# A two-layer attention kernel: a second tile for h1's copy and for h2, and every engine's order written out anew

## The reference

```python
# layer 0, per item
h  = rmsnorm(x) ;  h1 = x  + attention(h, h)            # "sa": 16 heads of 16, 256 keys
hn = rmsnorm(h1);  h2 = h1 + attention(hn, context)     # "ca": 77 keys
hn = rmsnorm(h2);  h3 = h2 + (silu(hn @ gate) * (hn @ up)) @ down     # inner width 1024
# layer 1, per item: norm_F = layernorm(h3), norm_X = layernorm(context)
a  = softmax(norm_F @ norm_X.T / 16) @ norm_X
c  = gelu(a @ fc1.T + fc1_b) @ fc2.T + fc2_b            # inner width 4
s  = attention of layernorm(c) with itself, one head
out = norm_F + gamma2 * (c + gamma1 * s)
```

## Time and profile before

| | us |
|---|---|
| median of 3 runs (lowest, highest) | 937.34 (936.94, 937.65) |
| span of the profiled execution | 938.1 |
| PE busy, weight loads busy | 869.7, 738.1 |
| DVE busy, ACT busy, POOL busy | 666.7, 546.2, 252.9 |
| mean granted TensorE clock | 0.984 |

### The profile page before, as it was taken

One profiled execution on the slowest core, in us unless ns is written; L12 is line 12 of the kernel. 1 busy time (PEld: TensorE's weight loads), 2 busy tenths in 40 slices (PEclk: granted clock), 3 DMA queues, 4 the chain that ended last, 5 costly groups with the idle time before them and its releaser, 6 DMA issues.

```text
span 938.1 us, 21220 instructions
## 1 busy us (share of the span) xinstructions
PE 869.7 (93%) x8114; PEld 738.1 (79%) x8114; DVE 666.7 (71%) x1445; ACT 546.2 (58%) x1098; POOL 252.9 (27%) x511
## 2 busy tenths in 40 slices
...
PEclk9899999999999999999999999999999999997999
...
GB/s 207 191 148 128 134 76 81 61 105 26 57 101 43 94 64 80 79 81 56 102 38 55 104 44 95 63 81 77 80 55 92 50 43 105 43 33 35 17 12 23
DMA packets 74660, 71.73 MB, mean 76 GB/s; under 512 B 17633, under 2 KB 67409, under 8 KB 74561
## 3 DMA queue, kind: packets, MB, share of 16 engines
...
...
## 4 chain that ended last, share of the span: by engine, by line
PE 74%; DVE 12%; ACT 6%; issue 3%; DMA 2%; SPq 1%; POOL 1%; ACTq 0%; DVEq 0%
PE mring L1527 21%; PE ring L1527 12%; PE down_ps L1667 9%; PE od L1634 9%; PE ring L1620 7%; PE ring L1600 6%; DVE mx_sa L1296 4%; PE ring L1535 2%; PE mring L1696 1%; PE mring L1769 1%; DVE late_a L1343 1%; ACT probs L1094 1%; PE ring L1607 1%; PE mring L1677 1%; DMA pk_sa<-qkT 1%
## 5 line engine op out<-in xcount | busy, mean ns | idle before, releaser
L1094 ACT ACTIVATE probs<-ring 128x1024 f32<-128x1024 f32 (+1 forms) x192 | 190.9, 1022 | 45.3 <-PE ring L1620 41.5
L849 POOL TENSOR_TENSOR hidT_lo<-late_a,hidT_hi 128x256 fp32r<-128x256 f32 x128 | 95.8, 750 | 316.9 <-ACT hidT_hi L1121 315.7
L1296 DVE TENSOR_REDUCE mx_sa<-ring 128x4 f32<-128x1024 f32 x128 | 153.4, 1215 | 11.4 <-PE ring L1600 11.3
L1301 DVE TENSOR_REDUCE mx_ca<-ring 128x4 f32<-128x308 f32 x128 | 55.1, 474 | 59.8 <-PE ring L1600 59.7
L1349 DVE SCALAR_TENSOR_TENSOR late_a<-late_a,mring 128x256 f32<-128x256 f32 x128 | 52.9, 413 | 49.1 <-ACT late_a L1111 48.7
L1667 PE MATMUL down_ps<-down_hi,hidT_hi 128*128 128x256 f32 x256 | 79.0, 309 | 0.0
L1111 ACT ACTIVATE late_a<-mring 128x256 f32<-128x256 f32 x128 | 48.4, 378 | 51.2 <-PE mring L1527 48.9
L1600 PE MATMUL ring<-pk_sa 63*128 63x256 f32 x512 | 62.8, 329 | 14.9 <-DVE mx_sa L1296 6.4
L1667 PE MATMUL down_ps<-down_lo,hidT_hi 128*128 128x256 f32 x256 | 71.3, 279 | 0.0
L1667 PE MATMUL down_ps<-down_hi,hidT_lo 128*128 128x256 f32 x256 | 71.3, 279 | 0.0
L1121 ACT ACTIVATE hidT_hi<-late_a 128x256 fp32r<-128x256 f32 x128 | 52.6, 413 | 27.0 <-DVE late_a L1351 19.9
...
## 6 DMA issues: line engine op xcount, KB each, us to landing
...
```

The lines of the kernel that those rows point to most:

```text
L849: nc.gpsimd.tensor_tensor(hidT[1][:, m % HID, :], hid[:, m % 2, :], hidT[0][:, m % HID, :].bitcast(F32), ALU.subtract).then_inc(S["hidlo"] ...
L1094: nc.scalar.activation(granule(g, tag)[0:rows_, i0:i0 + 2, :, :].rearrange("p i h t -> p h i t"), ring_tile(("E", tag, k))[0:rows_].rearra ...
L1296: nc.vector.tensor_reduce(mx[tag][:, :, :, k].rearrange("p q h -> p h q"), ps[:].rearrange("p h (q t) -> p h q t", t=T), AX_X, ALU.max).th ...
L1301: nc.vector.tensor_reduce(mx[tag][:, :, half, 2 * C * (k % 2) + k // 2:2 * C * (k % 2) + k // 2 + C + 1:C].rearrange("p q i -> p i q"), v, ...
```

## The change

- `h1_ca` gets a second tile (`h1_odd`), h2 a second one in `v_all`, which is free after the start. Even items use the first, odd items the second. The two waits above now look two items back.
- `ORDER` holds every (step, item) of every engine; `MOVED` and the sorting are gone. The steps are the same. Of TensorE's 1105, 784 have another place in the list, mostly by one to ten places.
- `MOVED_TILES` gives 62 `ring` and 91 `mring` fills the other PSUM tile.
- `IDLE` has 167 identity products, 100 of them ahead of items 0 to 2 (55 before) and 67 near the end (41 before).
- `w5_sb` shares the space of `lpT`.

Below, the lines of ORDER for DVE and TensorE around item 6 stand for the whole text; the start of ACT's and of DVE's list follow.

```diff
+ORDER["dve"]: S.sa.0@6 S.sa.1@6 o.ca.1@4 hv@0 wo.sa@5
+        oT.ca@4 S.sa.2@6 aT.ca@4 S.sa.3@6 ms.ca@5 wo.ca@4 s2@2 ms.mlp@4 xn.ca@5 xn.mlp@4 S.sa.4@6 T.mlp@4 S.sa.5@6 S.sa.6@6 u2@2 S.sa.7@6
+        maxsplit.sa@6 T.ca@5 gu.0@4 gu.1@4 ms.sa@7 lnstat.nx@4 qk.ca@5 dn@3 lnstat.nf@3 lncen.nf@3 gu.2@4 gu.3@4 S.ca.0@5 S.ca.1@5 sc@3 S.ca.2@5
...
+ORDER["pe"]: S.sa.0@6 S.sa.1@6 pv.ca.1@4 wo.sa@5 nXT@3 dnp.3@3 xT@2 S.sa.2@6 S.sa.3@6
+        dnp.4@3 dnp.5@3 dnp.6@3 wo.ca@4 s2@2 v.sa@6 mT2@2 S.sa.4@6 e2@2 dnp.7@3 T.mlp@4 u2@2 S.sa.5@6 S.sa.6@6 gu.0@4 S.sa.7@6 T.ca@5 gu.1@4 maxT.sa@6
+        qk.ca@5 gu.2@4 E.sa.0@6 E.sa.1@6 gu.3@4 E.sa.2@6 pv.sa.0@6 E.sa.3@6 E.sa.4@6 dnp.0@4 nFT@3 dnp.1@4 S.ca.0@5 S.ca.1@5 fT@2 sc@3 E.sa.5@6
...
+ORDER["act"], start: gT.0@0 norm.sa@0 ws.0@0 ws.1@0 T.sa@0 ws.2@0 norm.sa@1 ws.3@0 ws.4@0 ws.5@0 qk.sa@0
-    start before:    ws.0@0 gT.0@0 ws.1@0 ws.2@0 ws.3@0 norm.sa@0 ws.4@0 gk.0@0 gv.0@0 T.sa@0 ws.5@0 kt@0 gT.1@0 ws.6@0 qk.sa@0
+ORDER["dve"], start: gT.0@0 ms.sa@0 xn.sa@0 T.sa@0 ws.0@0 ws.1@0 ws.2@0 ws.3@0 ws.4@0 ws.5@0 qk.sa@0 S.sa.0@0
-    start before:    gT.0@0 ws.0@0 ws.1@0 km@0 ws.2@0 ws.3@0 ms.sa@0 ws.4@0 xn.sa@0 gk.0@0 T.sa@0 ws.5@0 gT.1@0 ws.6@0 qk.sa@0 kt@0 S.sa.0@0
...
+        h1_at = (h1_ca, sb("h1_odd", [P, QT, D]))
+        h2_at = (h2, v_all[:].rearrange("p q h e -> p (q h e)")[:, 0:QT * D].rearrange("p (q d) -> p q d", q=QT))
...
             def h1_for_ca(n):
                 act.wait_ge(S["sa", "res"].sem, S["sa", "res"].at(n, 1))
-                if not_first(n):
-                    act.wait_ge(S["ca", "res"].sem, S["ca", "res"].at(n - 1, 1))
+                if not_first(n, 2):
+                    act.wait_ge(S["ca", "res"].sem, S["ca", "res"].at(n - 2, 1))
...
-                nc.scalar.activation(h1_ca[:], h1[:], ACT.Copy).then_inc(S["h1"].sem, 1)
+                nc.scalar.activation(h1_at[n % 2][:], h1[:], ACT.Copy).then_inc(S["h1"].sem, 1)
...
-                src, dst = (x_res, h1) if tag == "sa" else (h1_ca, h2)
+                src, dst = (x_res, h1) if tag == "sa" else (h1_at[n % 2], h2_at[n % 2])
...
-                if tag == "ca" and not_first(n):
-                    dve.wait_ge(S["h3"].sem, S["h3"].at(n - 1, 1))
+                if tag == "ca" and n == 1:
+                    dve.wait_ge(s_vst, 16 * moves(len(GROUPS) - 1))
+                if tag == "ca" and not_first(n, 2):
+                    dve.wait_ge(S["h3"].sem, S["h3"].at(n - 2, 1))
```

More of the change, by code:

```diff
@@ L67 @@
[L67 to L70, removed]
+        gT.0@0 norm.sa@0 ws.0@0 ws.1@0 T.sa@0 ws.2@0 norm.sa@1 ws.3@0 ws.4@0 ws.5@0 qk.sa@0 ws.6@0 ws.7@0 gv.0@0 ws.8@0 ws.9@0 gk.0@0 v.sa@0 gT.1@0
@@ L79 @@
     "pe": """
[L80 to L83, removed]
@@ L309, in sequence, with step_of @@
[L309 to L326 removed]
+def step_of(word):
+    name, *args = word.split(".")
+    return (name, *(int(a) if a.isdigit() else a for a in args))
```

459 lines of the change are left out of this document (276 added, 183 removed), and 70 rows, old and new, of the table MOVED.

## The result

The changed kernel takes 929.08 us (median of 4 runs, 926.74 to 931.43), the kernel before 937.5 beside it: a ratio of 0.9907, interval 0.9884 to 0.993. It is faster, by 8.4 us. The forecast was 24 us, so the gain is a third of what was forecast. Two more measurements of the same kernel gave 928.23 and 927.28 us (ratios 0.9895 and 0.9897). Its 14 single times run from 922.5 to 935.9 us with a standard deviation of 3.9 us; the 68 of the kernel before run from 933.6 to 945.1 with 2.0. That wider spread turns out to be part of the story.

The account below looks back on a forecast made before the run. DVE's list was taken to bound the S stretch (S.sa.0 to maxT.sa done), some 40% of each item, PE the rest. Middle -16, start -5, end -3 give -24: 914.1 us span, 913.3 us time; forecast 906 to 922, 8-in-10 range 900 to 936.

Parts of the forecast that it names:

- The start, -5: Up to S.sa.0 of item 2: earlier norm.sa, ms.sa and xn, later gk, gv and fold; -5 us, ends -12 and +3.
- The whole shift and the identity products keep the clock: Best case for the start: qk.sa's full shift of at most 5.7 us counts and the clock holds; -12 us.
- The middle, -16: S stretches (S.sa.0 to maxT.sa done), items 2 to 15: three quarters of -21.5 us of DVE work and waits; ends -25, 0.
- DVE's list sets the S stretch: From S.sa.0 to maxT.sa done, some 40% of each item, DVE's work is the bound: busy 18.39 of 19.95 us.
- -12.0 us for dn and gu.0: DVE work leaving the S stretches: dn -6.8, gu.0 -8.3, less what enters; free in the other stretch.
- -9.5 us for the covered rstd waits: xn.ca and ms.ca between ms.mlp and xn.mlp cover two thirds of DVE's 1.02 us idle per item, 14 items.
- this is not a third gain: ACT running norm.ca ahead of norm.mlp, with mT2 and v.sa behind it, falls in the same S stretches; no extra gain.
- Its signs: If right: S stretches 18.0 to 18.9 us, DVE over 90% busy or PE without waits; wrong if 19.5 or more.
- Partly given back: Rival, 0.20: PE becomes the bound as its covers shrink; 8 to 12 us lost over 14 items, time 922 to 935.
- mT2 to e2: In that rival: PE work between these two kernel steps shrinks from 2.2 to 0.3 to 0.7 us; about 0.9 needed.
- Slower through mring: Rival, 0.10: 78 more consecutive fills on one PSUM tile wait for readers; 952 us at 0.5 us each.
- The end, -3: From wo.ca to T.mlp of items 14 and 15: more cover, 2 us wait and perhaps 2 us cold clock; ends -8, +1.

Follow-up runs that it names:

- after_b: The changed kernel unaltered, measured a third time: 927.28 us, ratio 0.9897.
- idle_both: Changed kernel with the 19 identity products of item 1 put back and those at the end as before (41, not 67): 926.75 us, ratio 0.9878.
- idle_item1: Changed kernel with the 19 identity products that the kernel before had in item 1 put back: 925.01 us, ratio 0.9835.
- half_before: Kernel before with the sa maxima taken over half of the keys, so DVE has less to do: 932.31 us.
- dn_late: Kernel before plus second tiles; in items 5 to 13 dn goes behind u2 on DVE, dnp.0 to just before dnp.1 on TensorE: 944.24 us, 1.0062.
- dve_part: Kernel before, second tiles; items 5 to 13: dn, dnp.0 and gu.0 later, h1, norm.ca, ms.ca and xn.ca earlier: 962.58 us.
- h1_early: Kernel before, second tiles; items 4 to 13: h1, norm.ca ahead of norm.mlp on ACT, ms.ca, xn.ca earlier on DVE: 940.44 us, 1.0021.
- cover1: Kernel before, second tiles; items 5 to 13: dn and dnp.0 later, dnp.7 moved between S.sa.4 and v.sa on TensorE: 942.43 us.
- after_again: The changed kernel unaltered, measured a second time: 928.23 us, ratio 0.9895.
- after: The changed kernel itself, first measurement and profile: 929.08 us, ratio 0.9907 to the kernel before.
- tail_idle: Changed kernel with the identity products at the end as in the kernel before (41, not 67): 925.66 us.
- half_after: Changed kernel with the sa maxima taken over half of the keys, so DVE has less to do: 917.95 us.
- idle_item1_b: Second measurement of the changed kernel with the 19 identity products of item 1 put back: 923.19 us.
- old_head: Old order and identity products up to S.sa.0 of item 2, the changed kernel's order, tiles and products from there on: 927.86 us.

## Why the prediction was wrong, point by point

- **The sum.** In the first profile the parts are +4.3, -7.1 and -5.7 us for -5, -16 and -3: the start and the middle each miss by some 9. The forecast took the clock of the kernel before as given outside the start and the end ("the granted clock is at full speed in nearly all slices"). It was not given: the missing products cost 5 to 8 us in item 1, and the low clock at 755 some 3 us in the first profile (item 14 takes 54.9 us, 52.0 in after_b). idle_both's parts are -2.8, -13.5 and -7.6, together -23.9 for -24. That agreement is luck. It is the fastest of six executions of a kernel with other products, set against a usual one of before; no part agrees by itself, and the middle's reason is wrong. At equal clock the changed kernel is 12 to 13 us faster, not 24 (below).
- **The clock and the times.** Changed kernel 922.5 us at a mean clock of 0.988, 928.5 at 0.979 and 935.9 at 0.970; before, 937.5 at 0.985, 938.8 at 0.978 and 945.1 at 0.968. A straight line through all executions gives 7.4 us for 0.01 of clock in the changed kernel (14 executions) and 4.4 before (64 of known clock). At 0.984 the lines give 925.3 and 937.4, at 0.988 922.4 and 935.7. That the fuller TensorE makes the low clock dearer fits this; it was not tested.
- **The start, -5: the step that failed.** "The whole shift and the identity products keep the clock" was counted as a chance of more gain. The new list has none of the 19 products of item 1, and the prediction only added up the totals, 100 for 55. It priced the products by the time that they take (0.24 us each) and put what they protect at nothing. It measured +2.0 to +5.7 us for -5 (113.3, 115.6 and 117.0 for 111.3), and -2.6 to -3.0 with the 19 products. The shift itself was right: S.sa.0 of 0 at 26.2 for 30.96. The Trainium skill (GPSIMD Engine Reference, section Key points) says that GpSimd shares its SBUF interfaces with VectorE. By that rule `fold` would take time back in item 1, 2 us by the prediction. It does not: the one operation of DVE beside it with two SBUF inputs, aT's low part (L1360), took 0.70 us for 0.69 before (0.78 in idle_item1), and sa_wo's split, now away from `fold`, 0.68 for 1.09.
- **The middle, -16: the mechanism was wrong.** It measured -7.1, -8.6 and -11.0 us in the changed kernel, -13.5 in idle_both. The step that failed is "DVE's list sets the S stretch", from 18.39 us busy in 19.95. DVE waited in between for what TensorE did in its own order, and 4.2 us of DVE work less shortened a stretch by 0.3 (half_before). -12.0 us for dn and gu.0: dn is worth 0 (dn_late), gu.0 was not parted from its tile (dve_part). -9.5 us for the covered rstd waits: DVE's idle time before xn.mlp did fall, from 10.6 us in 14 stretches to 3.3, as forecast, but such waits give 0.2 us a stretch (h1_early), some 3 us in 14. As far as the gain is explained, it comes from places in TensorE's list, of v.sa above all (cover1), and of v.sa and mT2 the prediction had said that "this is not a third gain".
- **Its signs did not part the theories.** DVE busy for over 90% of the S stretches, the wait before xn.mlp gone, ACT's wait for the residual sum down by over half (56.9 to 22.5 us), the weight-load share at 82%, S.sa.0 of 0 at 26.2, the clock at 1.00 from wo.ca of 14 on: all came true, and they hold as well if TensorE's order sets the stretch. The S stretches themselves, 19.1 us, fell between its two signs (up to 18.9, or 19.5 and more). Of the signs against it one came true, the longer start, though not "for `fold` and the later splits".
- **Partly given back.** This rival held in part. The other stretches of items 3 to 14 did not grow while the transfers were in time (some 379.6 us in idle_both for 380.1) and grew by 1.6 us in after_b. Excess rose ahead of S.ca.0 (0.6 us before, 2.7 in idle_both, 4.5 in after_again, in 12 items), ahead of qk.ca (0.2 to 2.1, from T.ca, a cover that the prediction had named) and, inside the S stretches, ahead of wo.ca (0.3 to 3.5). Two other named covers, nFT to sc and mT2 to e2, were not it. S.ca.0 of 11 in after_b and in idle_both:

```profile
648.46 0.52 PEld L1633 LDWEIGHTS ring<-kpk_ca,qpk_ca 63*128 63x128 f32 x8 [1.60 <-DMA qpk_ca<-qkT]
```

```profile
641.86 0.52 PEld L1635 LDWEIGHTS ring<-kpk_ca,qpk_ca 63*128 63x128 f32 x8 [0.41 <-issue]
```

The third packing transfer of ca of 11 lands 4.6 us after its issue in after_b and 2.7 in idle_both, and in the changed order it has no cover left. This is no chance of one execution: it takes 4.5 to 4.6 us in all five profiles of the changed order without the products in item 1 (after, after_again, after_b, tail_idle, half_after) and 2.7 in the other four that have the changed middle (idle_both, idle_item1, idle_item1_b, old_head). In the five, a 16 KB packet of the instruction queue (q8) takes 0.9 us on the DMA engines between issue and landing; in the four it is over before the issue. No experiment moved that packet alone.
- **Slower through mring.** It did not happen; 78 more pairs of fills on one tile cost nothing that shows in TensorE's waits. dve_part shows that the mechanism is real: 1.5 us a pair once the reader is late.
- **The end, -3.** Right in kind, mis-sized: -5.7 to -8.5. The low clock of item 14 cost 4 to 5 us between gu.0 and gu.4, not 2. The term for 18 products, +0.5, came to 0.5 to 0.8 (tail_idle).
